# Start of a fused two-layer kernel: text projected in two parts around the first transposes, half of the feature copies on VectorE

## What is computed

```
xn  = layernorm(x)                        # no weight, eps 1e-5
fp  = xn @ W;   tp = text @ Ws            # features 512 -> 512, text 64 rows a sequence
h   = tanh(tp[:, None, :, :] + fp[:, :, None, :] + b)   # every token with every text row
rho = h @ w;    att = softmax(rho + mask) over the 64 text rows
th  = att @ text
out = tanh(th @ Wcw + bcw) * xn + tanh(th @ Wcb + bcb)
x   = x + tanh(g) * out
```

## Time and profile before

| | us |
|---|---|
| median of 3 runs | 1945.01 |
| lowest to highest | 1943.3 to 1946.8 |
| the profiled execution, its own time | 1944.79 |
| its span in the trace | 1942.8 |

### The profile page before, as it was taken

The page is one execution under the profiler, slowest core; times in us unless marked ns, Lnnn a source line. Parts: engine busy times, 40 slices in busy tenths (PEclk is TensorE's granted clock), DMA queues, the critical chain, the costliest instruction groups (busy, mean ns, idle before and its releaser), DMA issues.

```text
span 1942.8 us, 24516 instructions
## 1 busy us (share of the span) xinstructions
PE 1597.1 (82%) x9510; PEld 719.8 (37%) x9510; DVE 1711.3 (88%) x2606; ACT 1481.7 (76%) x1105; POOL 613.9 (32%) x480
## 2 busy tenths in 40 slices
PE   6868965788556976786489987999999987899996
PEld 4212211122111321231144434666666653444442
DVE  6889998999999998889689886899999867999997
ACT  4899999999999999999644665454545336888781
POOL 1000000000000000000044225666666644899991
PEclk9999999999999999999889998999999999999999
DMA  5000200011000010000079765233333111122212
GB/s 203 1 1 23 87 12 0 23 52 41 6 1 1 17 49 12 1 3 10 0 248 354 262 221 155 92 115 109 99 115 100 56 55 40 45 77 76 66 55 76
DMA packets 116709, 143.65 MB, mean 74 GB/s; under 512 B 25326, under 2 KB 74606, under 8 KB 116210
## 3 DMA queue, kind: packets, MB, share of 16 engines
q1 hardware_dynamic: 116594, 142.10, 22.1%
HBM read 87.55 MB, written 50.33 MB: 71 GB/s over the span
## 4 chain that ended last, share of the span: by engine, by line
ACT 43%; PE 35%; DVE 13%; POOL 4%; issue 3%; DMA 2%; SPq 0%; DVEq 0%; POOLq 0%; ACTq 0%
ACT unit L514 40%; PE psum L1681 5%; PE psum L1715 5%; PE psum L1018 4%; PE psum L1012 4%; PE psum L1667 3%; DVE unit L423 2%; POOL h L1856 2%; PE psum L1738 2%; PE psum L1691 2%; PE psum L1708 2%; DVE psum L1447 1%; DVE psum L1452 1%; POOL hidden L1873 1%; PE psum L1700 1%
## 5 line engine op out<-in xcount | busy, mean ns | idle before, releaser
L514 ACT ACTIVATE unit<-unit 128x4096 f32<-128x4096 f32 x244 | 857.4, 3608 | 0.5 <-DVE unit L423 0.3
L423 DVE TENSOR_SCALAR unit<-feat_proj,text_proj 128x1024 f32<-128x1024 f32 x976 | 667.2, 746 | 67.1 <-PE psum L639 65.3
L639 PE MATMUL psum<-unit,w_pad 128*32 128x512 f32 x3904 | 474.6, 604 | 234.0 <-ACT unit L514 234.0
L639 PEld LDWEIGHTS psum<-unit,w_pad 128*32 128x32 f32 x3904 | 102.5, 109 | 556.9 <-ACT unit L514 398.7
L680 POOL TENSOR_SCALAR red<-red 128x8 f32<-128x8 f32 x4 | 2.0, 508 | 531.5 <-DVE red L321 531.5
L1738 PE MATMUL psum<-xq_block,w_q 128*128 128x512 bf16 x512 | 123.2, 386 | 14.2 <-ACT h L1614 11.0
L1856 POOL TENSOR_TENSOR h<-h,arow 128x512 f32<-128x512 f32 x104 | 125.8, 1233 | 20.1 <-ACT h L1614 20.1
L680 POOL TENSOR_SCALAR rstd<-mv 128x8 f32<-128x8 f32 (+1 forms) x5 | 1.7, 333 | 411.9 <-DVE mv L216 411.9
L547 PE MATMUL psum<-xnT,W_sb 128*128 128x512 f32 x256 | 125.2, 617 | 2.1 <-ACT xnT L465 2.1
L1589 ACT ACTIVATE scores<-scores 128x1024 f32<-128x1024 f32 x32 | 33.9, 1058 | 114.0 <-POOL scores L1842 114.0
L1873 POOL TENSOR_TENSOR hidden<-hidden,srow 128x2048 f32<-128x2048 f32 x28 | 114.3, 4084 | 9.8 <-DVE hidden_q L1482 9.7
(11 more groups left out here) (256 smaller groups left out, 2754.0 us busy)
## 6 DMA issues: line engine op xcount, KB each, us to landing
h_scratch<-h SPq DMA_DIRECT2D x44, 512.0 KB, 4.8
hin<-h_scratch SPq DMA_DIRECT2D x32, 704.0 KB, 4.6
xin<-in_x SPq DMA_DIRECT2D x8, 1024.0 KB, 6.7
tern_in<-in_w1T SPq DMA_DIRECT2D x16, 512.0 KB, 4.7
tern_in<-in_w2T SPq DMA_DIRECT2D x16, 512.0 KB, 6.2
x<-in_x SPq DMA_DIRECT2D x16, 512.0 KB, 3.7
x_scratch<-x SPq DMA_DIRECT2D x32, 256.0 KB, 2.0
x3in<-x_scratch SPq DMA_DIRECT2D x31, 256.0 KB, 3.0
```

The source lines that it names most:

```text
L423: ins = ve.tensor_scalar(units[:, n % 3, k, :], FP[:, bi % 2, k, :], TP[:, k, n:n + 1], None, ALU.add)
L514: ac.activation(units[:, n % 3], units[:, n % 3], ACT.Tanh).then_inc(unit_tanh, 1)
L639: mm = te.matmul(psum[k * TG:(k + 1) * TG, 3 + 2 * grp + half, :], w_pad[:, k, TG - 1 - tt:2 * TG - 1 - tt], units[:, n % 3, k, half * BAN ...
```

## The change

It does seven things. (1) Of the text only the 64 rows of batch 0 are projected at the start, and ahead of the first transposes (`text_first`, 64 columns in place of 256), so ScalarE copies 64 columns a quarter. (2) The other 192 columns are projected in slots 13, 14, 16 and 17 of the unit loop, and the two text rows in slots 18, 20, 21 and 22 in halves; VectorE copies them out in slots 19, 22 and 27. (3) Batch 0's transposes alternate between banks 0 and 7, so a turn waits for the copy of the last but one. (4) VectorE takes the largest values of tiles 0 to 3 after normalising (tile 0's ahead of the fourth normalise), the moments of tiles 4 to 7 after those, and normalises tiles 4 and 5 after the adds of the first quarter, 6 after the second's, 7 after the third's (before: 4 to 6 ahead of the ramp, 7 after the first quarter). TensorE turns 4 and 5 after the second projection, 6 after the third and 7 after the fourth (before: 4 to 7 after the first to the fourth), and ScalarE copies them out there. (5) The four copies of the second half's projections go from ScalarE to VectorE, behind the adds of half units 6, 8, 9 and 11. (6) SyncE issues `w` and `b` directly behind the first tiles, ahead of the text, `Ws` and `W`. (7) ScalarE takes a first sigmoid at once, so the table is loaded at the start, and the two gate activations move behind the first ramp block; GpSimd clears `v_diag` at the start.

```diff
+    TURN0_BANK = (0, 7)
+    NORMALISED_AFTER = ((4, 5), (6,), (7,), ())
+    TURNED_AFTER = ((), (4, 5), (6,), (7,))
+    TEXT_REST = (13, 14, 16, 17)
+    TEXT_ROWS = (18, 20, 21, 22)
+    TEXT_LAG = 5
+    PROJECTED_AFTER = (6, 8, 9, 11)
+    TEXT_DONE = 2 * KC + 2
+
+    def rest_bank(m):
+        return psum[:, 5 + m // 2, m % 2 * (NU - TXT):(m % 2 + 1) * (NU - TXT)]
 
 ...
+        def text_rest(n):
+            for m in (1, 3):
+                if n == TEXT_REST[m] + TEXT_LAG:
+                    V.wait_ge(text_mm, KC + m + 1)
+                    V.wait_ge(early_loaded, NEARLY)
+                    for c in (m - 1, m):
+                        ins = ve.tensor_scalar(TP[:, c, TXT:NU], rest_bank(c), small[:, 1, c:c + 1], None, ALU.add)
+                    ins.then_inc(text_copied, 2)
+            if n == TEXT_ROWS[-1] + TEXT_LAG:
+                V.wait_ge(text_mm, 2 * KC + 2)
+                for r, row in enumerate((cw_row, cb_row)):
+                    ins = ve.tensor_copy(row[:, :], psum[:, 7, r * NU:(r + 1) * NU])
+                ins.then_inc(text_copied, 2)
+
 ...
-        for q in range(2):
-            for i in range(q * TPK, (q + 1) * TPK):
-                moments(0, i)
-            aggregate(0, q * TPK, (q + 1) * TPK)
-            for i in range(q * TPK, (q + 1) * TPK - q):
-                normalise(0, i)
-                if i <= TPK:
-                    largest(0, i)
+        for i in range(TPK):
+            moments(0, i)
+        aggregate(0, 0, TPK)
+        for i in range(TPK):
+            if i == TPK - 1:
+                largest(0, 0)
+            normalise(0, i)
+        for i in range(1, TPK):
+            largest(0, i)
+        for i in range(TPK, TPB):
+            moments(0, i)
+        aggregate(0, TPK, TPB)
 ...
             for u in range(SLOTS):
                 ramp_add(u, k, k + 1)
-            if k == 0:
-                normalise(0, TPB - 1)
-            else:
-                largest(0, TPK + k)
+            for i in NORMALISED_AFTER[k]:
+                normalise(0, i)
+            largest(0, TPK + k)
             moments(1, k)
 ...
             i = u - SLOTS
+            if u in PROJECTED_AFTER:
+                j = KC + PROJECTED_AFTER.index(u)
+                V.wait_ge(fp_mm, j + 1)
+                ve.tensor_copy(FP[:, 0, j - KC, BANK:2 * BANK], psum[:, FP0_BANK[j], :]).then_inc(fp_copied, 1)
 ...
-        for i in range(TPK):
-            turned(i)
+        A.wait_ge(ident_done, 1)
+        ac.activation(sig[:, :], half_neg[:, 0:2], ACT.Sigmoid)
         A.wait_ge(early_loaded, NEARLY)
         for m in range(KC):
             A.wait_ge(text_mm, m + 1)
-            ac.activation(TP[:, m, :], psum[:, 3 + m, 0:NU], ACT.Identity, bias=small[:, 1, m:m + 1]).then_inc(text_copied, 1)
+            ac.activation(TP[:, m, 0:TXT], psum[:, 3 + m, 0:TXT], ACT.Identity,
+                          bias=small[:, 1, m:m + 1]).then_inc(text_copied, 1)
+        for i in range(TPK):
+            turned(i)
+        for k in range(KC):
+            projected(k)
+            for i in TURNED_AFTER[k]:
+                turned(i)
+            for u in range(SLOTS):
+                ramp_tanh_of(u, k, k + 1)
         A.wait_ge(const_loaded, NCONST)
         ac.activation(sig[:, :], clips[:, :], ACT.Sigmoid).then_inc(gates_done, 1)
         ac.activation(tg[:, :], gates[:, :], ACT.Tanh).then_inc(gates_done, 1)
-        for k in range(KC):
-            projected(k)
-            turned(TPK + k)
-            for u in range(SLOTS):
-                ramp_tanh_of(u, k, k + 1)
-        for j in range(KC):
-            projected(KC + j)
-            for u in range(SLOTS + 2 * j, SLOTS + 2 * j + 2):
-                ramp_tanh_of(u, 0, KC)
-        for u in range(SLOTS + 2 * KC, 2 * RAMP):
+        for u in range(SLOTS, 2 * RAMP):
             ramp_tanh_of(u, 0, KC)
-            if u == 2 * RAMP - 4:
-                for r, row in enumerate((cw_row, cb_row)):
-                    A.wait_ge(text_mm, KC + r + 1)
-                    ac.activation(row[:, :], psum[:, 7, r * NU:(r + 1) * NU], ACT.Copy).then_inc(text_copied, 1)
 
 ...
-        def text_rows():
-            T.wait_ge(const_loaded, NCONST)
-            for r in range(2):
-                for k in range(KC):
-                    mm = te.matmul(psum[:, 7, r * NU:(r + 1) * NU], small[:, 2 + r, k:k + 1].broadcast_to([P, P]),
-                                   ctx_sb[:, k, :], start=(k == 0), stop=(k == KC - 1))
-                mm.then_inc(text_mm, 1)
+        def text_first(m):
+            T.wait_ge(text_loaded, 32)
+            for k in range(KC):
+                mm = te.matmul(psum[:, 3 + m, 0:TXT], Ws_sb[:, k, m * P:(m + 1) * P], ctx_sb[:, k, 0:TXT],
+                               start=(k == 0), stop=(k == KC - 1))
+            mm.then_inc(text_mm, 1)
+
+        def text_rest(n):
+            for m, at in enumerate(TEXT_REST):
+                if n == at:
+                    T.wait_ge(text_copied, KC)
+                    for k in range(KC):
+                        mm = te.matmul(rest_bank(m), Ws_sb[:, k, m * P:(m + 1) * P], ctx_sb[:, k, TXT:NU],
+                                       start=(k == 0), stop=(k == KC - 1))
+                    mm.then_inc(text_mm, 1)
+            for j, at in enumerate(TEXT_ROWS):
+                r, part = divmod(j, 2)
+                if n == at:
+                    T.wait_ge(const_loaded, NCONST)
+                    T.wait_ge(xnT_copied, TPB)
+                    for k in (2 * part, 2 * part + 1):
+                        mm = te.matmul(psum[:, 7, r * NU:(r + 1) * NU], small[:, 2 + r, k:k + 1].broadcast_to([P, P]),
+                                       ctx_sb[:, k, :], start=(k == 0), stop=(k == KC - 1))
+                    if part == 1:
+                        mm.then_inc(text_mm, 1)
 
         def turn(bi, i):
             t = bi * TPB + i
             T.wait_ge(ident_done, 1)
             T.wait_ge(xn_done, t + 1)
-            T.wait_ge(xnT_copied, t)
+            T.wait_ge(xnT_copied, t if bi else t - 1)
+            bank = 0 if bi else TURN0_BANK[i % 2]
 ...
+        for m in range(KC):
+            text_first(m)
         for i in range(TPK):
             turn(0, i)
-        T.wait_ge(text_loaded, 32)
-        for m in range(KC):
-            for k in range(KC):
-                mm = te.matmul(psum[:, 3 + m, 0:NU], Ws_sb[:, k, m * P:(m + 1) * P], ctx_sb[:, k, :],
-                               start=(k == 0), stop=(k == KC - 1))
-            mm.then_inc(text_mm, 1)
         for k in range(KC):
             project(0, k, 0, KC)
-            turn(0, TPK + k)
+            for i in TURNED_AFTER[k]:
+                turn(0, i)
         for j in range(KC):
             project(0, KC + j, 0, KC)
             ramp_rho(2 * j)
             ramp_rho(2 * j + 1)
-        text_rows()
 ...
         load_x(0, 0)
+        for dst, src in ((small[:, 0, :], w), (small[:, 1, :], b)):
+            sp.dma_start(dst, src).then_inc(early_loaded, 16)
         sp.dma_start(ctx_sb[:, :, :], ctxT).then_inc(text_loaded, 16)
         sp.dma_start(Ws_sb, Ws).then_inc(text_loaded, 16)
         sp.dma_start(W_sb[:, :, :], W).then_inc(W_loaded, 16)
-        for dst, src in ((small[:, 0, :], w), (small[:, 1, :], b)):
-            sp.dma_start(dst, src).then_inc(early_loaded, 16)
```

More of the change, by code:

```diff
@@ L294, in tail @@
                 if s == at:
-                    V.wait_ge(text_copied, KC + 2)
+                    V.wait_ge(text_copied, TEXT_DONE)
                     V.wait_ge(tail_step, done + ATT_INV + 2 * n)
@@ L419, in vector_A @@
             V.wait_ge(unit_mm, n - 2 - RAMP)
+            if n == TXT:
+                V.wait_ge(text_copied, 2 * KC)
             if n < RAMP + 3:
@@ L430, in vector_A @@
                 prep(bi + 1, t)
+            text_rest(n)
             weights(n)
@@ L464, in turned @@
             A.wait_ge(xnT_filled, i + 1)
-            ac.activation(xnT[:, :, i * P:(i + 1) * P], psum[:, 0, :].rearrange("p (k t) -> p k t", k=KC),
+            ac.activation(xnT[:, :, i * P:(i + 1) * P],
+                          psum[:, TURN0_BANK[i % 2], :].rearrange("p (k t) -> p k t", k=KC),
                           ACT.Copy).then_inc(xnT_copied, 1)
@@ L530, in turn @@
             T.wait_ge(xn_done, t + 1)
-            T.wait_ge(xnT_copied, t)
+            T.wait_ge(xnT_copied, t if bi else t - 1)
+            bank = 0 if bi else TURN0_BANK[i % 2]
             for k in range(KC):
-                tr = te.transpose(psum[:, 0, k * P:(k + 1) * P], xn[:, t % 3, k * P:(k + 1) * P], ident[:, :])
+                tr = te.transpose(psum[:, bank, k * P:(k + 1) * P], xn[:, t % 3, k * P:(k + 1) * P], ident[:, :])
             tr.then_inc(xnT_filled, 1)
@@ L564, in rho_sum @@
             T.wait_ge(start_step, 2)
-            T.wait_ge(text_copied, KC + 2)
+            T.wait_ge(text_copied, TEXT_DONE)
             T.wait_ge(tail_step, (bi - 1) * TAIL_STEPS + RHO_MASKED)
@@ L675, in gpsimd_A @@
         G.wait_ge(ident_done, 1)
```

(2 more changed lines are left out.)

## The result

The changed kernel takes 1937.67 us, the median of 6 runs (1933.62 to 1939.65), against 1944.99 before (6 runs, 1943.3 to 1946.94). The ratio is 0.9956, its 95% interval 0.9944 to 0.9968: 0.4% faster, 7.3 us by the medians. The profiled execution took 1936.77, with a span of 1934.9.

What follows compares the result with a forecast made beforehand. ScalarE's unit tanh was taken to bound the unit loop, so only its start at 92.9 us could move: 6.3 - 0.7 + 1.8 + 2.6 = 10.0 us off 1944.8, median 1935.0 us, range 1932.5 to 1939.8.

Steps and rivals of the forecast that it cites:

- first rival: Start: clock stays low until the features; gain there 1.9 us in place of 6.3, total 1939.4 us; chance 16%.
- first case: The summed outcome: 10.0 us gained, 1935.0 us, own range 1932.6 to 1937; chance 51%.
- The start of the text: TensorE's start: text begins when `Ws` lands, at 10.9 us, with 0.6 us for `w` and `b` ahead.
- The text: Start: 32 matmuls of 64 columns take 6.0 us, the first 3.6 us at the low clock level.
- Turns and copies: Behind the text: four turns on two banks and their copies take 3.3 us; first feature projection at 20.2 us.
- The first half's order: Ramp's first half: two tile copies follow in quarter two, one of them bare; cost 0.7 us.
- The clock at the second half: First projection of second half: shorter TensorE gap keeps clock up, 3.63 us in place of 5.40; gain 1.8 us.
- second rival: Second half: the clock falls there all the same, so gain is 8.2 us in all, 1936.8 us; chance 17%.
- Copies on VectorE: Second half: moving four projection copies off ScalarE lets half unit 12's add start earlier; gain 0.7 us.
- Text rows out of the ramp: Ramp: ScalarE is spared 1.24 us of wait before half unit 14 and 0.65 of copies; gain 1.9 us.
- third rival: Ramp: VectorE bounds it, all four copies on its path; 2.7 us lost, 1937.7 us; chance 7%.
- The unit loop: Slots with added text work: TensorE and VectorE have room, ScalarE does not wait; cost zero.

Runs made afterwards that it cites:

- e9: The changed kernel unaltered, run again on the same chip as two others: 1937.35 us, ratio 0.9959; unit tanh from 86.54 us.
- e7: The changed kernel with the issue of `w` and `b` moved back behind `W`: unit tanh from 84.81 us.
- e4: The changed kernel with 28 idle matmuls of 128 columns ahead of the text, while TensorE waits for `Ws`: text 3.8 us, unit tanh from 80.23 us.
- e3: The kernel before with 8 idle matmuls filling TensorE's 2.1 us gap ahead of the second half: projection there 3.70 us, unit tanh from 92.24 us.
- e11: The kernel before with only batch 0's turns alternating between two banks: first projection at 23.6 us, unit tanh from 88.40 us.
- e1: The changed kernel with the second half's four copies back on ScalarE: unit tanh from 85.19 us, 45.17 us after the second half's first projection.
- e2: The changed kernel with the two text rows back in the ramp, their copies on ScalarE: unit tanh from 87.36 us.
- e10: The changed kernel with the turns ahead of the narrow text, as in e6, timed: 1935.6 us, ratio 0.9946; unit tanh from 81.78 us.
- e6: The changed kernel with the four turns (two banks) ahead of the narrow text: first projection at 18.8 us, unit tanh from 81.58 us.
- e5: The changed kernel with all 256 text columns ahead of the turns, none in the unit loop: text 8.7 us, unit tanh from 85.28 us.
- e8: The changed kernel with 28 idle matmuls during the wait for `Ws` and text quarters between the turns: 1931.32 us, ratio 0.9928.

## Why the prediction was right

The time lies in the range, faster was the likeliest outcome, and the start of the unit tanh was put at 82.9 (92.9 less 10.0) and came at 84.3, in e9 at 86.5. The range was made wide enough to hold the first rival's 1939.4 too, and the result lies in that added part: 1937.67 is above 1937, the upper end that the prediction gave its first case (its own bound of 24.8 for the first projection would put that end at 1939.6). The gain was 7.3 us by the medians where 10.0 was summed. Step by step:

- *The start of the text*: 10.9 was given, 10.5 measured. The 0.6 us for `w` and `b` can't be seen (e7).
- *The text*: the term that was mis-sized. The step took "3.6 us at twice 0.125 (14 of them) and the other 18 at 0.135: 6.0 us". It was 7.1, all of it at the low level: 0.215 each. The price at the high level, put at 0.125 to 0.135, was not far off (0.113, e4). The assumption that the level would rise during the 64-column matmuls, as it had during the 256-column ones, was wrong in all five traces with the narrow text in front (7.09 us in each). That is the first rival's mechanism, given 16%, and it held up to the turns; of the turns' 5.1 and the projection's 1.8 us that this rival also charged, the first trace shows 3.9 and nothing, e9 4.4 and the 1.8. So e9 is nearer to that rival than to the first case, and that the median stayed well inside the range is in part luck: the two traces differ in when the level rose.
- *Turns and copies*: 3.3 given, 3.9 measured to the last hand-over. Together, the first projection at 21.5 in place of 20.2, 4.9 us earlier than before by the timeline (21.50 against 26.37).
- *The first half's order*: 0.7 given. From the first to the second half's projection it is 18.1, against 17.8 in all four traces of the old order: 0.3.
- *The clock at the second half*: 1.8 given and, by e3, 1.7. But the shorter gap is a guard and not the only cause, as e11 shows, and the second rival (17%) was a fair one.
- *Copies on VectorE*: 0.7 given, 0.5 by e1. *Text rows out of the ramp*: 1.9 given, 2.4 by e2, since the wait ahead of half unit 14 grows when half unit 12 starts earlier. Together 2.6 given and, by the tails, 47.04 - 44.69 = 2.35 measured. The parts don't add: bringing the rows back costs all of it, bringing the copies back 0.5. VectorE as the bound of the ramp (the third rival, 2.7 us lost) did not come.
- *The unit loop*: zero given, and ScalarE's idle time there is 0.5 us before and after.

In the first trace these come to 4.87 - 0.32 + 1.70 + 2.35 = 8.60 us, the whole of what the unit tanh gained. The new order on VectorE and the early sigmoid were not run alone; they are in the first two terms.

The term the prediction did not question is the reason for the new order. It weighed the text's price but not what would have been there had the turns stayed in front. By e11 the second bank alone is worth 2.8 us at the first projection; the second bank and the narrow text together, turns in front, 7.4 to 7.6 (e10, e6); with the text in front 4.9 (4.4 in e9). The parts don't add: narrowing gives 0.4 to 0.9 us where the text comes first (e5 against the five traces with the narrow text), and 4.6 to 4.8 where it comes behind the turns (e6 and e10 against e11, which also lacks the new order on VectorE and SyncE).

The Trainium skill ("TensorE: Matmul & The Clock Gate", section "Wait — 56ns, not 53.3ns?") has matmuls start every N columns divided by the clock plus 2.5 ns, down to a floor near 25 ns. The prediction set that against a row, and for the 64 columns of this change the runs side with the row. Start to start at the high level, in the middle of a run of instructions, the traces have 0.429 us at 512 columns (L598), 0.216 at 256 (e5's text), 0.163 at 192 (L563) and 0.109 at 128 (the turns of e4). These agree with the Trainium skill's rule if the columns of each of these 32-bit instructions are counted twice: 2 x 256 columns at 2.4 GHz and 2.5 ns would be 0.216 by it. Below 128 columns the time stops falling: 0.112 at 64 (e4) and 0.112 at 32, far above the Trainium skill's floor. At the low level it is 0.213 at 64 columns (L554) as at 128 (the first turns behind them). All of these have a full load of 32-bit weights of 128x128; that the load sets this floor is likely, but no run here has narrower weights.

## What to carry to other kernels

Ahead of a stretch that TensorE sets, ask at which clock level it will run, and try the wider matmuls in front of the narrow ones, not behind them: here five traces ran the 64-column text at the low level to its end, while with the turns' 128 columns in front it was at the high level from its first matmul (e6) or after 0.9 us (e10). Where TensorE must wait for a load anyway, idle matmuls that end as the load lands brought the unit tanh 4 us forward here (e4), and with the text between the turns 6.0 us in time (e8). Narrowing a 32-bit matmul below 128 columns bought nothing while its weights stayed full; at 192 and 256 the columns counted. And when parts of a change share a resource, run them in both orders: here the second bank and the narrowing carried the gain, and the reordering took a third of it back (7.5 and 4.9 us at the first projection).

## What the runs showed that I had not expected

- In the clock column of a window the first microseconds read 1.00 while the durations show the low level: 22 to 24 us in e9 is printed at 1.00, and there the projections' matmuls last 1061 to 1194 ns and 3 of them stand where 26 to 28 us, at 592 ns, has 6 (columns: length, busy time and count of PE, PEld, DVE, ACT, POOL, clock, DMA).

```profile
22.00:24.00 2.00, 2.00 (x3) 0.97 (x4) 1.70 (x8) 0.00 (x0) 0.23 (x1) 1.00 1.05 407
...
26.00:28.00 2.00, 2.00 (x6) 0.93 (x5) 0.00 (x0) 0.53 (x1) 0.00 (x0) 1.00 0.06 22
```

- One and the same program starts its unit loop at 84.3 or 86.5, by when the level rises, and the rest of the kernel scatters by 2.9 us more. Together that could make up most of the 6.0 us between the fastest and the slowest of the changed kernel's first six runs; with two traces of it this is not shown. e8, which brings the level up before anything waits for it, has 2.2 us between its five, but so has the changed kernel in e9 (2.05), so a narrower spread of e8 is not shown either.
